# Moving the gamma LayerNorm's apply from two VectorE passes to two GpSimd passes and one VectorE pass

## The chip, the cores and the metric

The program runs on all 8 cores of one Trainium2 chip. Each core takes two of the 16 batch entries, and no core talks to another. The metric is the device time of the slowest core in microseconds (us). The engines are called as in the profile: PE is TensorE, DVE is VectorE, ACT is ScalarE, POOL is GpSimd, SP is the engine that issues the weight loads.

## The reference

The input is x of 16 x 2048 x 1024 floats. Three residual sublayers follow each other; the weights of the two FFNs are the same.

```python
def _layernorm(x, axis=-1, eps=1e-5): ...
x = x + 0.5 * _L0_ffn_ref(_layernorm(x), W1, b1, W2, b2, scale)
x = x + _L0_attn_ref(_layernorm(x), gamma, w_qkv, w_out)
x = x + 0.5 * _L0_ffn_ref(_layernorm(x), W1, b1, W2, b2, scale)
```

The FFN is a 1024 to 4096 to 1024 network with GELU, and with a small token-dependent term (rank 4) added to each of its two products. The attention has 8 heads of 128, is causal, and normalises its input once more by its root mean square and by gamma:

```python
l2 = jnp.sqrt(jnp.sum(x * x, axis=-1, keepdims=True))
xn = x / jnp.maximum(l2, 1e-12) * scale_norm * gamma
```

## The kernel before

Everything is held transposed: channels lie on the 128 partitions in 8 groups (cc), tokens along the free dimension. R is the residual in f32 (8 x 2048 columns), xn the normalised input in bf16, arena the 8 MB of hidden activations or of Q, K and V. The program handles one sequence of 2048 tokens after the other, and each as FFN 1, attention, FFN 2.

A list scheduler is not used. The builder calls emit in the order in which the work is written, each engine runs its own list strictly in that order, and waits come from the buffers' records of readers and writers. So the place of a call in the code sets the order on every engine.

ffn (from L741) runs two tiles of 1024 tokens (ti), each with an up projection (L762, GELU at L780) and two passes (nh) of 512 tokens: u, the small term's factor, is formed by 32 thin matmuls (L799), copied out of PSUM by ACT (L808), sent through DRAM and back, and beside it 256 matmuls of the down projection (L831) fill all eight PSUM banks. The pass ends with L845, ACT's bias (L852, into f32t) and DVE's residual add (L860). After each pass a hook is called.

ln_block (from L470) normalises one block of 512 tokens. PE sums x (L474) into PSUM bank 6; POOL or ACT squares each channel group into one of two halves of sqt (L488), and PE sums the squares (L494) into bank 7; ACT reads the sums (L504, L508), DVE and ACT form the variance and its inverse root in rows (L512 to L529), ACT sends two rows to DRAM and has them broadcast to 128 partitions as rep_a (scale) and rep_b (minus mean times scale). Then, for each of the 8 channel groups, two passes apply them, through the single buffer f32t. In the plain LayerNorm that a hook runs these are POOL's (L578, L582). With gamma fused they are DVE's (L585, L590): f32t = R * gamma * rep_a, then xn = rep_b * gamma + f32t.

The order around the change comes from FFN 1's hook, in its second tile:

```python
elif ti == 1 and nh == 0:
    ln_block(0, True, sq_eng='pool')
    ln_block(512, True, sq_eng='pool')
    ln_block(NT, True, sq_eng='pool')
elif ti == 1 and nh == 1:
    ln_block(NT + 512, True, sq_eng='pool')
```

So three blocks are normalised between the two down passes of the second tile, and the fourth behind the second pass, ahead of attention. Attention begins with V (L952): 16 tiles of 128 tokens, each 8 matmuls into one of two PSUM banks, copied out by DVE (L967); the first 12 tiles need no xn of the fourth block. These four calls, made for both sequences, are the only ones with gamma fused.

Of the kernel before, what the change touches and what calls it, by code (L numbers as in the profile page):

```python
# [251 lines left out]
def build(n_sub=3):  # L252
# [25 lines left out]
    p = Prog(nc)  # L278
    bufs = {}
    ctx = contextlib.ExitStack()  # L280
    with ctx:
        def sb(name, shape, dtype, nslots=1):
            t = ctx.enter_context(nc.sbuf_tensor(name, shape, dtype))
            bufs[name] = Buf(nslots)
            return t

        R = sb("R", [128, CC * S], F32, nslots=32)
# [5 lines left out]
        f32t = sb("f32t", [128, 512], F32)  # L293
        ln_t = f32t
# [17 lines left out]
        rep_a = sb("rep_a", [128, 512], F32)  # L312
        rep_b = sb("rep_b", [128, 512], F32)
# [4 lines left out]
        gamc = sb("gamc", [128, CC], F32)  # L318
# [21 lines left out]
        def B(name):  # L340
            return bufs[name]

        def rsl(cc, t0_, w=512):
            return R[:, cc * S + t0_: cc * S + t0_ + w]

        def rslot(cc, t0_):
            return cc * 4 + t0_ // 512

        def xsl(cc, t0_, w=512):
            return xn[:, cc * S + t0_: cc * S + t0_ + w]  # L350
# [27 lines left out]
        for name in ("b1c", "b2c", "gamc", "onesc", "onesf", "onesr", "negr", "ident",  # L378
# [3 lines left out]
                        deps=[ini_tok], group="scb", tag="scbc")  # L382
        B("scol").wrote(t_sc_ev)
        for src_s, dst_s, nm in ((o1s, o1sc, "o1sc"), (o2s, o2sc, "o2sc")):
            t = p.emit("dve", lambda e, src_s=src_s, dst_s=dst_s: e.tensor_scalar_mul(
                dst_s[:, :], src_s[:, :], scol[:, 0:1]),
                deps=[t_sc_ev, ini_tok], tag=nm)
# [78 lines left out]
        def layer_norm(t0, ntok, gamma_fused, bcast_pe=False, sq_eng="act"):  # L466
            for n0 in range(t0, t0 + ntok, 512):
                ln_block(n0, gamma_fused, bcast_pe, sq_eng)

        def ln_block(n0, gamma_fused, bcast_pe=False, sq_eng="act"):  # L470
            if True:
                ta = tb = None
                for cc in range(CC):
                    t_sa = p.emit("pe", lambda e, cc=cc, n0=n0: e.matmul(  # L474
                        ps[6][0:1, :], onesf[:, :], rsl(cc, n0), start=(cc == 0), stop=(cc == CC - 1)),
                        deps=B("R").deps_read(rslot(cc, n0)) + B("onesf").deps_read() +
                             (B("ps6").deps_write() if cc == 0 else []),
                        tag="sumx")
# [3 lines left out]
                for cc in range(CC):  # L482
# [4 lines left out]
                    else:  # L487
# [3 lines left out]
                        deps=B("R").deps_read(rslot(cc, n0)) + B("sqt").deps_write(pr), tag="sq")  # L491
# [5 lines left out]
                        deps=[t_sq] + B("onesc").deps_read() + (B("ps7").deps_write() if cc == 0 else []),  # L497
                        tag="sumx2")
# [6 lines left out]
                              deps=[ta] + B("srow_a").deps_write(), tag="mu")  # L505
# [3 lines left out]
                              deps=[tb] + B("srow_b").deps_write(), tag="ex2")  # L509
# [3 lines left out]
                             deps=[t_ea] + B("srow_c").deps_write(), tag="mu2")  # L513
# [3 lines left out]
                             deps=[t_eb, t_c], tag="var")  # L517
# [12 lines left out]
                              deps=[t_rsd, t_ea] + B("srow_c").deps_write(), tag="murstd")  # L530
# [3 lines left out]
                if bcast_pe:  # L534
                    t_b1m = p.emit("pe", lambda e: e.matmul(ps[6][:, :], onesr[:, :], srow_b[:, :],
                                                            start=True, stop=True),
                                   deps=[t_rsd] + B("ps6").deps_write() + B("onesr").deps_read(),
                                   tag="bcp1")
# [3 lines left out]
                    t_bc1 = p.emit("act", lambda e: e.copy(rep_a[:, :], ps[6][:, :]),  # L542
                                   deps=[t_b1m] + B("rep_a").deps_write(), tag="bcp1e")
# [5 lines left out]
                                   deps=[t_mr] + B("ps7").deps_write() + B("negr").deps_read(),  # L549
                                   tag="bcp2")  # L550
# [3 lines left out]
                    t_bc2 = p.emit("act", lambda e: e.copy(rep_b[:, :], ps[7][:, :]),  # L554
                                   deps=[t_b2m] + B("rep_b").deps_write(), tag="bcp2e")
                    B("ps7").read(t_bc2)
                    B("rep_b").wrote(t_bc2)
                else:
                    t_neg = p.emit("dve", lambda e: e.tensor_scalar_mul(srow_c[:, :], srow_c[:, :], -1.0),
                                   deps=[t_mr], tag="negmur")  # L560
# [7 lines left out]
                    t_bc1 = p.dma("act", rep_a[:, :], browL[0:1, 0:512].broadcast_to([128, 512]),  # L568
                                  deps=[t_o1] + B("rep_a").deps_write(), group="browL", tag="brL1i")
                    B("rep_a").wrote(t_bc1)  # L570
                    t_bc2 = p.dma("act", rep_b[:, :], browL[0:1, 512:1024].broadcast_to([128, 512]),
                                  deps=[t_o2] + B("rep_b").deps_write(), group="browL", tag="brL2i")
                    B("rep_b").wrote(t_bc2)
                ap_eng = "pool" if (sq_eng == "pool" and not gamma_fused) else "dve"
                for cc in range(CC):
                    xslot = rslot(cc, n0)
                    if not gamma_fused:
                        t_p1 = p.emit(ap_eng, lambda e, cc=cc, n0=n0: e.tensor_mul(  # L578
                            ln_t[:, :], rsl(cc, n0), rep_a[:, :]),
                            deps=[t_bc1] + B("f32t").deps_write() + B("R").deps_read(rslot(cc, n0)),  # L580
                            tag="lnap1")
                        t_p2f = lambda e, cc=cc, n0=n0: e.tensor_add(  # L582
                            xsl(cc, n0), rep_b[:, :], ln_t[:, :])
                    else:
                        t_p1 = p.emit(ap_eng, lambda e, cc=cc, n0=n0: e.scalar_tensor_tensor(  # L585
                            ln_t[:, :], rsl(cc, n0), gamc[:, cc:cc + 1], rep_a[:, :],
                            ALU.mult, ALU.mult),
                            deps=[t_bc1] + B("f32t").deps_write() + B("R").deps_read(rslot(cc, n0)) +
                                 B("gamc").deps_read(), tag="lnap1g")
                        t_p2f = lambda e, cc=cc, n0=n0: e.scalar_tensor_tensor(  # L590
                            xsl(cc, n0), rep_b[:, :], gamc[:, cc:cc + 1], ln_t[:, :],
                            ALU.mult, ALU.add)
                    B("rep_a").read(t_p1)
                    B("R").read(t_p1, rslot(cc, n0))
                    B("f32t").wrote(t_p1)
                    t_p2 = p.emit(ap_eng, t_p2f,
                                  deps=[t_bc2, t_p1] + B("xn").deps_write(xslot), tag="lnap2")
                    B("rep_b").read(t_p2)
                    B("f32t").read(t_p2)
                    B("xn").wrote(t_p2, xslot)  # L600
# [278 lines left out]
        def attn(ln_pre_blocks=0, hook=None):  # L879
            for n0 in range(ln_pre_blocks * 512, S, 512):  # L880
                ln_block(n0, True)
# [317 lines left out]
        for seq in range(BPC):  # L1199
            if n_sub >= 3:  # L1200
                first = (seq == 0)

                def ffn1_hook(ti, nh):
                    if ti == 0 and nh == 0:
                        if not first:
                            ln_block(NT, False, sq_eng='pool')
                            ln_block(NT + 512, False, sq_eng='pool')
                        t1_compute(NT)
# [6 lines that stand above are left out]
# [35 lines left out]
            else:  # L1250
# [9 lines left out]
               deps=B("srow_c").deps_write(), tag="trail_nop_act")  # L1260
# [47 lines left out]
```

How the kernel before makes its waits and increments, by code:

```python
            def run(engine_obj):  # L128
                hiwater = {}
                for op in oplist:
                    waits = {}
                    for d, m in op.deps:
                        if elided(e, d):
                            continue
                        s, v = d.sem, d.val
                        if m:
                            mo = margin_tok(d, op)
                            if mo is not None and mo.dma_group is None:
                                s, v = mo.tok.sem, mo.tok.val
                        assert s is not None, (e, op.tag, d.eng, d.idx)
                        if hiwater.get(s, 0) >= v:
                            continue
                        if waits.get(s, 0) < v:
                            waits[s] = v
                    for s, v in waits.items():
                        engine_obj.wait_ge(get_sem(s), v)
                        hiwater[s] = v
                        stats["waits"] += 1
                    ins = op.fn(engine_obj)
                    if op.needs_inc:
                        amt = 16 if op.dma_group is not None else 1
                        ins.then_inc(get_sem(op.tok.sem), amt)
                        stats["incs"] += 1
```

## Time and profile before

| what | value |
|---|---|
| timed runs | 4866.82 and 5091.31 us, median 4979.07 |
| the profiled execution | 4859.01 us |
| its span, slowest core (of 4834.5 to 4857.2) | 4857.2 us |
| PE busy | 3765.5 us, 78% of the span |
| ACT busy | 1206.7 us, 25% |
| POOL busy | 615.5 us, 13% |
| DVE busy | 597.4 us, 12% |
| chain that ended last, by engine | PE 64%, DMA 15%, ACT 5%, DVE 5%, issue 5%, POOL 5% |
| mean granted TensorE clock, eight cores | 0.872 to 0.875 of full speed |

The span runs from the first to the last instruction of one core; the 2 us beside it are the start and end of the program. An engine's busy time does not say what it holds up: the chain and the waits do. The eight cores do the same work and differ by half a per cent. The profile and all its rows are those of the slowest core, core 3.

### The profile page before, as it was taken

The numbers are of one execution on the slowest core, as the hardware profiler recorded it, in microseconds if no ns is written. First come the engines' busy times: TensorE is split into PE (matmuls) and PEld (weight loads), VectorE is DVE, ScalarE is ACT, GpSimd is POOL, SyncE is SP. The second block draws the span as 40 slices with busy tenths as digits, with TensorE's granted clock in tenths as the row PEclk, the third lists the DMA queues.
The fourth block names the chain that finished last, engine by engine and source line by source line (L and its number), as shares of the span: only waits on it lengthen the run. The fifth ranks groups of instructions, "written<-read, shape, count | busy, mean of one in ns | idle before, by whom it ended". The sixth has DMA issues, their size and how long they took to land.

```text
span 4857.2 us, 44500 instructions; the slowest of 8 cores (4834.5 to 4857.2 us)
## 1 busy us (share of the span) xinstructions
PE 3765.5 (78%) x14592; PEld 1310.6 (27%) x14592; DVE 597.4 (12%) x887; ACT 1206.7 (25%) x1873; POOL 615.5 (13%) x594
## 2 busy tenths in 40 slices
PE   5058999668888857896949849967878777597997
PEld 1013333222232212332313313322212212133333
DVE  3000001330031020000000010042112111100000
ACT  2012031015515502202212212210343344131121
POOL 0000001010010054002030040020110111610000
PEclk8579999878898978998969969988889989698998
DMA  9962423300100101252324213312010010023434
GB/s 191 196 134 59 121 58 87 87 14 18 42 11 18 33 11 40 61 153 71 92 74 122 70 42 94 79 57 76 20 37 14 18 31 18 14 61 96 113 81 130
DMA packets 436609, 333.30 MB, mean 69 GB/s; under 512 B 321130, under 2 KB 325612, under 8 KB 436388
## 3 DMA queue, kind: packets, MB, share of 16 engines
q1 hardware_dynamic: 394612, 252.00, 19.5%
q0 software_dynamic: 18144, 50.34, 5.2%
q10 hardware_dynamic: 23632, 28.12, 2.0%
q8 instruction: 126, 2.06, 0.2%
q14 instruction: 95, 0.78, 0.1%
HBM read 313.07 MB, written 42.45 MB: 73 GB/s over the span
## 4 chain that ended last, share of the span: by engine, by line
PE 64%; DMA 15%; ACT 5%; DVE 5%; issue 5%; POOL 5%; ACTq 1%; DVEq 0%; SPq 0%; POOLq 0%
PE ps L762 19%; PE ps L831 17%; PE ps L981 4%; PE ps L773 3%; PE ps L1051 3%; PE ps L1061 3%; PE ps L799 2%; PE ps L952 2%; PE ps L1028 2%; DVE nrm L903 2%; POOL sqt L488 2%; DMA browF<-srow_a 2%; PE ps L1154 2%; POOL xn L582 2%; POOL f32t L578 1%
## 5 line engine op out<-in xcount | busy, mean ns | idle before, releaser
L762 PE MATMUL ps<-xn,wb 128*128 128x512 bf16 x4096 | 986.3, 384 | 127.4 <-DMA wb<-w1s 113.2
L831 PE MATMUL ps<-arena,wb 128*128 128x512 bf16 x4096 | 895.7, 380 | 60.9 <-ACT u L808 51.0
L831 PEld LDWEIGHTS ps<-arena,wb 128*128 128x128 bf16 x4096 | 397.0, 98 | 558.6 <-issue 94.7
L780 ACT ACTIVATE arena<-ps,b1c 128x512 bf16<-128x512 f32 x512 | 351.4, 687 | 714.5 <-PE ps L773 700.3
L762 PEld LDWEIGHTS ps<-xn,wb 128*128 128x128 bf16 x4096 | 361.3, 98 | 618.8 <-issue 262.2
L1038 ACT ACTIVATE pb<-ps,negm 128x512 bf16<-128x512 f32 x640 | 419.2, 686 | 222.4 <-PE ps L1028 128.8
L860 DVE SCALAR_TENSOR_TENSOR R<-f32t,R 128x512 f32<-128x512 f32 x128 | 95.4, 746 | 2511.3 <-ACT f32t L852 1846.7
L488 POOL TENSOR_TENSOR sqt<-R 128x512 bf16<-128x512 f32 x160 | 176.1, 1131 | 1490.4 <-PE ps L494 827.3
L852 ACT ACTIVATE f32t<-ps,b2c 128x512 f32<-128x512 f32 x128 | 88.0, 687 | 1007.6 <-PE ps L845 899.0
L1051 PE MATMUL ps<-pb,onesc 128*1 128x512 bf16 x640 | 259.5, 406 | 89.7 <-ACT pb L1038 89.7
L494 PE MATMUL ps<-sqt,onesc 128*1 128x512 bf16 x192 | 92.1, 492 | 256.7 <-POOL sqt L488 249.2
L1028 PE MATMUL ps<-arena 128*128 128x512 bf16 x640 | 260.0, 416 | 30.6 <-ACT pb L1038 30.6
L889 POOL TENSOR_TENSOR sqt<-arena 128x512 bf16<-128x512 bf16 x128 | 132.2, 1038 | 1121.2 <-PE ps L981 954.7
L1061 PE MATMUL ps<-pb,arena 128*128 128x512 bf16 x640 | 266.5, 416 | 3.0 <-DVE arena L1089 3.0
L981 PE MATMUL ps<-xn,wb 128*128 128x512 bf16 x1024 | 234.3, 389 | 10.3 <-ACT arena L1000 10.3
L474 PE MATMUL ps<-R,onesf 128*1 128x512 f32 x384 | 197.3, 667 | 51.2 <-DMA R<-xT 36.7
L773 PE MATMUL ps<-t,e1z 4*128 4x512 bf16 x512 | 198.4, 388 | 0.0
L70 POOL DMA_DIRECT2D outT<-R x64 | 34.9, 546 | 1051.1 <-DVE R L860 1049.8
L723 PE MATMUL ps<-xn,o1c 128*4 128x512 bf16 x160 | 64.3, 563 | 128.0 <-ACT t L732 61.0
L1154 PE MATMUL ps<-arena 128*128 128x512 bf16 x512 | 131.8, 420 | 35.1 <-DVE arena L1089 27.0
L1051 PEld LDWEIGHTS ps<-pb,onesc 128*1 128x1 bf16 x640 | 50.7, 79 | 380.5 <-issue 380.5
L952 PE MATMUL ps<-arena,xn 128*128 128x512 bf16 x512 | 119.5, 398 | 43.0 <-DVE arena L967 43.0
(90 smaller groups left out, 2049.8 us busy)
## 6 DMA issues: line engine op xcount, KB each, us to landing
wb<-w2s SPq DMA_DIRECT2D x512, 256.0 KB, 2.6
wb<-w1s SPq DMA_DIRECT2D x256, 256.0 KB, 2.9
f32t<-browF ACTq DMA_DIRECT2D x64, 256.0 KB
outT<-R POOLq DMA_DIRECT2D x64, 256.0 KB, 3.3
arena<-w1T POOLq DMA_DIRECT2D x4, 2048.0 KB, 29.9
w1s<-arena SPq DMA_DIRECT2D x4, 2048.0 KB, 15.8
arena<-w2T POOLq DMA_DIRECT2D x4, 2048.0 KB, 25.7
w2s<-arena SPq DMA_DIRECT2D x4, 2048.0 KB, 16.3
```

What stands on the lines that cost most here:

```text
L488: sqf = lambda e, cc=cc, n0=n0, pr=pr: e.tensor_mul(sqt[:, pr * 512:(pr + 1) * 512], rsl(cc, n0), rsl(cc, n0))
L762: t_mm = p.emit("pe", lambda e, cc=cc, n0=n0, wt=wt, bank=bank: e.matmul(bank[:, :], wt[:, cc * 128:(cc + 1) * 128], xsl(cc, n0), start=(c ...
L773: t_c1 = p.emit("pe", lambda e, hc=hc, nh=nh, bank=bank: e.matmul(bank[:, :], e1z[:, hc * 128:(hc + 1) * 128], t1[:, nh * 512:(nh + 1) * 5 ...
L780: t_g = p.emit("act", lambda e, hc=hc, nh=nh, bank=bank: e.activation(h_act(hc, nh), bank[:, :], AF.Gelu, bias=b1c[:, hc:hc + 1]), deps=[t ...
L831: t_mm = p.emit("pe", lambda e, oc=oc, hc=hc, nh=nh, wt=wt, bank=bank: e.matmul(bank[:, :], wt[:, oc * 128:(oc + 1) * 128], h_act(hc, nh), ...
L952: t_mm = p.emit("pe", lambda e, cc=cc, tt=tt, bank=bank: e.matmul(bank[:, :], xn[:, cc * S + tt * 128: cc * S + (tt + 1) * 128], arena[:, ...
L981: t_mm = p.emit("pe", lambda e, cc=cc, nb=nb, wt=wt, bank=bank: e.matmul(bank[:, :], wt[:, cc * 128:(cc + 1) * 128], xsl(cc, nb * 512), st ...
L1028: t_s = p.emit("pe", lambda e, kcol=kcol, qcol=qcol, bank=bank, diag=diag: e.matmul(bank[:, :], arena[:, kcol:kcol + 128], arena[:, qcol:q ...
L1038: t_e = p.emit("act", lambda e, pslot=pslot, h=h, bank=bank: e.activation(pb[:, pslot * 512:(pslot + 1) * 512], bank[:, :], AF.Exp, bias=n ...
L1051: t_rs = p.emit("pe", lambda e, pslot=pslot, first=first, last=last, rsb=rsb: e.matmul(rsb[0:1, :], onesc[:, :], pb[:, pslot * 512:(pslot ...
L1061: t_pv = p.emit("pe", lambda e, vcol=vcol, pslot=pslot, first=first, last=last, ob=ob: e.matmul(ob[:, :], arena[:, vcol:vcol + 128], pb[:, ...
L1154: t_mm = p.emit("pe", lambda e, fc=fc, oc=oc, ocol=ocol, bank=bank: e.matmul(bank[:, :], arena[:, KT0 + fc * 1024 + oc * 128: KT0 + fc * 1 ...
```

## The change

For a block with gamma fused whose squares are POOL's, which is each of the four blocks of a sequence, the apply of one channel group is now three passes: POOL multiplies R by rep_a into f32t, POOL adds rep_b in place, and DVE multiplies the result by the group's column of gamma and writes xn in bf16. Since gamma is a factor of both terms, the result is the same up to rounding. The old branch stays in the code and is no longer reached.

```diff
                         t_p2f = lambda e, cc=cc, n0=n0: e.tensor_add(
                             xsl(cc, n0), rep_b[:, :], ln_t[:, :])
+                    elif sq_eng == "pool":
+                        t_p0 = p.emit("pool", lambda e, cc=cc, n0=n0: e.tensor_mul(
+                            ln_t[:, :], rsl(cc, n0), rep_a[:, :]),
+                            deps=[t_bc1] + B("f32t").deps_write() + B("R").deps_read(rslot(cc, n0)),
+                            tag="lnap0g")
+                        B("rep_a").read(t_p0)
+                        B("R").read(t_p0, rslot(cc, n0))
+                        B("f32t").wrote(t_p0)
+                        t_p1 = p.emit("pool", lambda e: e.tensor_add(
+                            ln_t[:, :], ln_t[:, :], rep_b[:, :]),
+                            deps=[t_p0, t_bc2], tag="lnap1g2")
+                        B("rep_b").read(t_p1)
+                        B("f32t").wrote(t_p1)
+                        t_p2f = lambda e, cc=cc, n0=n0: e.tensor_scalar_mul(
+                            xsl(cc, n0), ln_t[:, :], gamc[:, cc:cc + 1])
                     else:
                         t_p1 = p.emit(ap_eng, lambda e, cc=cc, n0=n0: e.scalar_tensor_tensor(
```

ln_t is another name of f32t. The second pass t_p2 is emitted on DVE as before.

POOL, from the weight preparation to the first attention, before. The squares (L488) of all four gamma blocks are one run of 32; L889 are the squares that attention takes of Q and K:

```order
L70 DMA arena<-wqkvT 128x2x3072 x4
L70 DMA arena<-woutT 128x4x1024 x2
L488 TENSOR_TENSOR sqt<-R 128x512 x32
L889 TENSOR_TENSOR sqt<-arena 128x512 x64
L488 TENSOR_TENSOR sqt<-R 128x512 x8
```

POOL in the changed kernel, around the end of block 0's apply and the squares of block 512. L585 is the new multiply, L592 the new add:

```order
L585 TENSOR_TENSOR f32t<-R,rep_a 128x512
L592 TENSOR_TENSOR f32t<-f32t,rep_b 128x512
L488 TENSOR_TENSOR sqt<-R 128x512 x8
L585 TENSOR_TENSOR f32t<-R,rep_a 128x512
L592 TENSOR_TENSOR f32t<-f32t,rep_b 128x512
```

Eight pairs now stand between the squares of one block and those of the next.

DVE before, at the end of block 0's apply and the statistics of block 512:

```order
L585 SCALAR_TENSOR_TENSOR f32t<-R,gamc,rep_a 128x512
L590 SCALAR_TENSOR_TENSOR xn<-rep_b,gamc,f32t 128x512
L512 TENSOR_TENSOR srow_c<-srow_a 1x512
L516 TENSOR_TENSOR srow_b<-srow_b,srow_c 1x512
L521 TENSOR_SCALAR srow_b<-srow_b 1x512
L529 TENSOR_TENSOR srow_c<-srow_a,srow_b 1x512
L559 TENSOR_SCALAR srow_c<-srow_c 1x512
L585 SCALAR_TENSOR_TENSOR f32t<-R,gamc,rep_a 128x512
```

DVE in the changed kernel, at the same place. L597 is the new multiply by gamma:

```order
L597 TENSOR_SCALAR xn<-f32t,gamc 128x512 x8
L512 TENSOR_TENSOR srow_c<-srow_a 1x512
L516 TENSOR_TENSOR srow_b<-srow_b,srow_c 1x512
L521 TENSOR_SCALAR srow_b<-srow_b 1x512
L529 TENSOR_TENSOR srow_c<-srow_a,srow_b 1x512
L559 TENSOR_SCALAR srow_c<-srow_c 1x512
L597 TENSOR_SCALAR xn<-f32t,gamc 128x512 x8
```

The statistics keep their place behind the block's apply; of the sixteen passes between them eight are left.

## Rows read from the trace of the kernel before

**Rows 1.** Groups by line, DVE then POOL: busy us, mean ns, idle before.

```profile
L585 DVE SCALAR_TENSOR_TENSOR f32t<-R,gamc,rep_a 128x512 f32<-128x512 f32 x64 | 52.6, 822 | 42.7 <-DMA rep_a<-browL 36.8
...
L521 DVE TENSOR_SCALAR srow_b<-srow_b 1x512 f32<-1x512 f32 x24 | 10.0, 415 | 2.6
...
L488 POOL TENSOR_TENSOR sqt<-R 128x512 bf16<-128x512 f32 x160 | 176.1, 1131 | 1490.4 <-PE ps L494 827.3 <-PE ps L723 250.7 <-PE ps L1154 212.3
...
L578 POOL TENSOR_TENSOR f32t<-R,rep_a 128x512 f32<-128x512 f32 x96 | 122.4, 1275 | 138.9 <-DMA rep_a<-browL 126.8
```

**Rows 2.** Waits of PE over the whole span: us in total, times, longest us.

```profile
PE ps L831 <- ACT u L808: 51.0, 2, 25.8
PE ps L952 <- DVE arena L967: 43.0, 2, 21.5
```

**Rows 3.** Timeline, first sequence: start us, us, engine, line, operation, [idle before].

```profile
844.13 1.26 DVE L590 SCALAR_TENSOR_TENSOR xn<-rep_b,gamc,f32t 128x512 bf16<-128x512 f32 x1 [2.18 <-DMA rep_b<-browL]
...
854.91 8.61 POOL L488 TENSOR_TENSOR sqt<-R 128x512 bf16<-128x512 f32 x6 [7.18 <-PE ps L494]
...
861.10 1.52 DVE L512 TENSOR_TENSOR srow_c<-srow_a 1x512 f32<-1x512 f32 x1
...
864.04 8.41 PE L799 MATMUL ps<-arena,o2c 128*4 128x512 bf16 x32
...
887.73 0.75 DVE L590 SCALAR_TENSOR_TENSOR xn<-rep_b,gamc,f32t 128x512 bf16<-128x512 f32 x1 [0.17 <-DVE f32t L585]
...
897.60 0.35 ACTq L70 DMA_DIRECT2D rep_b<-browL  x1
...
898.83 7.46 PE L831 MATMUL ps<-arena,wb 128*128 128x512 bf16 x21 [25.83 <-ACT u L808]
```

**Rows 4.** Timeline, second sequence, same place.

```profile
3215.91 1.49 DVE L590 SCALAR_TENSOR_TENSOR xn<-rep_b,gamc,f32t 128x512 bf16<-128x512 f32 x1 [1.95 <-DMA rep_b<-browL]
...
3270.20 49.59 PE L831 MATMUL ps<-arena,wb 128*128 128x512 bf16 x222 [25.18 <-ACT u L808]
```

**Rows 5.** Timeline ahead of attention, first sequence, then second.

```profile
981.75 0.59 ACT L508 ACTIVATE srow_b<-ps 1x512 f32<-1x512 f32 x1 [6.98 <-PE ps L494]
...
991.16 0.35 ACTq L70 DMA_DIRECT2D rep_b<-browL  x1
...
995.05 0.75 DVE L590 SCALAR_TENSOR_TENSOR xn<-rep_b,gamc,f32t 128x512 bf16<-128x512 f32 x1 [3.11 <-DMA rep_b<-browL]
...
1007.51 0.75 DVE L590 SCALAR_TENSOR_TENSOR xn<-rep_b,gamc,f32t 128x512 bf16<-128x512 f32 x1 [0.17 <-DVE f32t L585]
...
1009.01 26.55 PE L952 MATMUL ps<-arena,xn 128*128 128x512 bf16 x112 [21.52 <-DVE arena L967]
...
3364.47 0.75 DVE L590 SCALAR_TENSOR_TENSOR xn<-rep_b,gamc,f32t 128x512 bf16<-128x512 f32 x1 [2.49 <-DMA rep_b<-browL]
...
3377.00 0.75 DVE L590 SCALAR_TENSOR_TENSOR xn<-rep_b,gamc,f32t 128x512 bf16<-128x512 f32 x1 [0.24 <-DVE f32t L585]
```

**Rows 6.** Timeline of a plain LayerNorm that POOL applies, and the squares behind it.

```profile
1746.57 1.26 POOL L582 TENSOR_TENSOR xn<-rep_b,f32t 128x512 bf16<-128x512 f32 x1 [1.83 <-DMA rep_b<-browL]
...
1747.98 1.26 POOL L578 TENSOR_TENSOR f32t<-R,rep_a 128x512 f32<-128x512 f32 x1
...
1767.71 8.02 POOL L488 TENSOR_TENSOR sqt<-R 128x512 bf16<-128x512 f32 x8
...
1776.56 0.59 ACT L508 ACTIVATE srow_b<-ps 1x512 f32<-1x512 f32 x1 [24.03 <-PE ps L494]
```

**Rows 7.** Timeline: a residual add on DVE, and the POOL square waiting for it.

```profile
962.08 0.69 DVE L860 SCALAR_TENSOR_TENSOR R<-f32t,R 128x512 f32<-128x512 f32 x1 [0.88 <-ACT f32t L852]
...
963.04 1.04 POOL L488 TENSOR_TENSOR sqt<-R 128x512 bf16<-128x512 f32 x1 [99.52 <-DVE R L860]
```

**Rows 8.** Windows at PE's restart: PE, PEld, DVE, ACT, POOL busy us; PEclk, DMA share, GB/s.

```profile
890.00:905.00 15.00, 6.17 (x16) 2.07 (x17) 5.22 (x8) 3.26 (x6) 0.00 (x0) 0.52 0.20 55
905.00:920.00 15.00, 15.00 (x71) 6.83 (x70) 8.26 (x11) 0.00 (x0) 0.00 (x0) 1.00 0.48 142
```

## The prediction

> **What bounds the kernel now.** I read the groups by line first, to price the moved arithmetic. The first of the two DVE passes that apply a gamma LayerNorm block takes 0.82 us on average and runs 64 times [rows 1], the second as often. DVE as a whole is busy 12% of the span, so its load is no bound. TensorE (PE) carries the longest share of the chain that ended last, and what matters is where it stands still. The second view is therefore who waited for whom: PE waited 51.0 us in two waits for ACT's copies of u, and 43.0 us in two waits for DVE's copies of V [rows 2]. Both belong to the stage that the change touches. The third view is the timeline of that stage. I call the four blocks by their first token: 0, 512, 1024, 1536.
>
> *Place A*, between the two down projections of FFN 1's second tile: statistics of blocks 0, 512 and 1024 follow each other. Block 0's second apply pass starts when rep_b lands (844.13), DVE is done with block 0 only when it takes up block 512's mean at 861.10, its apply of block 512 ends at 888.48 (887.73 + 0.75), and only then can block 1024's variance start. ACT issues block 1024's broadcasts, the last at 897.60, and copies u behind them, so PE resumes at 898.83 after 25.83 us of idle time [rows 3]. The second sequence repeats it: 3215.91 to 3270.20 [rows 4]. *Place B*, ahead of attention: DVE applies block 1536 from 995.05 to 1008.26, and V's evacuations are queued behind it on DVE, so PE stands still 21.52 us until 1009.01 [rows 5]. So a longer apply lengthens the kernel at both places, in both sequences.
>
> **The change, part by part.** It removes 128 two-input DVE passes (8 blocks by 8 channel groups by 2) and adds 64 multiplies and 64 adds on POOL and 64 single-input multiplies on DVE. PE, the DMAs and ACT issue the same instructions.
>
> *Price of one channel group.* POOL's same multiply in the plain LayerNorm takes 1.26 us and the next dependent POOL instruction starts 1.41 us after it began (1747.98 minus 1746.57) [rows 1, 6]; the add takes 1.26 us. DVE's scalar multiply of 128x512 is not in the trace. The nearest row below is the 1x512 f32 scalar operation, 0.415 us, the nearest above the two-input pass, 0.75 us [rows 1, 5]; I take 0.42, since it is the same kind of operation over as many elements per partition, and keep 0.75. Now two handovers: there is one buffer f32t, so POOL's next multiply waits for DVE to have read it. DVE to POOL measured 0.27 us (962.08 + 0.69 to 963.04) [rows 7]; POOL to DVE is not shown, and the nearest row is DVE's wait for its own result, 0.17 us [rows 5]. I take 0.17 and 0.22 (the middle for the second), and keep zero and 0.27 for both as ends. One group then takes 1.41 + 1.26 + 0.17 + 0.415 + 0.22 = 3.47 us, against 1.78 before ((1007.51 - 995.05) / 7) [rows 5]. Counted from the landing of rep_b, POOL is free after 7 x 3.47 + 1.26 = 25.55 us and DVE after another 0.17 + 0.42, 26.15 us; before it was 13.21.
>
> The Trainium skill, "VectorE: DVE Perf Modes", section on the perf-mode tier table, lets an fp32 tensor_scalar in SBUF handle two elements per cycle where tensor_tensor handles one. By its fixed term of about 150 cycles my estimate is (256 + 151) / 0.96 GHz = 0.424 us; with the 0.75 us of a pass without that mode the total below would be about 15 us higher. No row shows this shape.
>
> *Place B.* POOL is idle there before the apply, and its squares come first in its queue. The last block is applied from the same moment and ends 26.15 - 13.21 = 12.9 us later; V's copies and PE follow one for one. Second sequence: (3377.00 + 0.75 - 3364.47) = 13.28 before, so again 12.9 [rows 5].
>
> *Place A.* Here the order decides. Before, POOL ran all squares without a stop (those of block 1024 from 854.91, while DVE applied block 0) [rows 3]. Now the squares of block 512 are queued on POOL behind the apply of block 0, those of 1024 behind the apply of 512; PE's sums of squares wait for them, then the statistics, then the next broadcast. Nothing overlaps any more. From block 0's rep_b at 844.13: apply 25.55; squares until ACT reads their sum 8.85 (1767.71 to 1776.56, a place where POOL is also the one waited for) [rows 6]; statistics and broadcast 13.3 (981.75 to 995.05) [rows 5]; apply of 512, 25.55; squares of 1024, 8.85; statistics to the last broadcast issue 9.41 (981.75 to 991.16) [rows 5]; u's copies and PE's start 1.23 (897.60 to 898.83) [rows 3]. Sum 92.74, so PE resumes at 936.9 instead of 898.83: 38.1 later. Second sequence: 3215.91 + 92.74 = 3308.65 against 3270.20, 38.4. The u matmuls (8.41 us from 864.04) [rows 3] now lie behind the last squares, 926.1 to 934.5, just inside ACT's chain, so they cost nothing; that cover is 2.4 us thin. They bring something back: at present PE restarts after its idle time at a granted clock of 0.52, the lower level (1.2 GHz), and is at 1.00 from 905 on [rows 8]; 21 matmuls took 7.46 us where 222 took 49.59 in the other sequence [rows 3, 4], a loss of 2.8 us. With u's matmuls immediately ahead, PE may be at full clock already. I take 1 us back in each sequence: 37.1 and 37.4.
> Block 1024's apply (926.25 + 13.3 to about 966) stays beside the down projection, which still has f32t unused until its end near 995; it costs nothing.
>
> A gain stands against this: DVE's passes took longer beside POOL's squares (six of them 8.61 us, against eight in 8.02 with no apply on DVE) [rows 3, 6]. The Trainium skill, "GPSIMD Engine Reference", Key points, says that POOL shares its SBUF interfaces with VectorE and contends with its two-input passes; by that rule the trace agrees and taking the passes off DVE frees the squares. It is in the sum already, since I took the undisturbed 8.85 us; with the disturbed rate of 8.61 / 6 per square it would be about 14 us more in total.
>
> **Sum.** 37.1 + 37.4 + 12.9 + 12.9 = 100.3 us. The profiled execution took 4859.01 us (span 4857.2), so about 4959 us, 2.06% more. The timed runs of before were 4866.82 and 5091.31, median 4979.07, so the profiled one lies 8 us under the lower; my figure is meant against the profiled and the lower one. 2%, about what a measurement of this kernel can tell from no change, is 97 us: the forecast lies almost on it.
>
> **Bounds.** Per sequence 21 group periods count. Handovers at zero give 3.09 us a period, 42 x 0.38 = 16 us less; the clock loss wholly recovered (2.8 instead of 1 in each sequence) 4 less: 4939. Handovers of 0.27 and a DVE pass of 0.75 give 3.96, 21 us more; u's matmuls wholly at 1.2 GHz (32 x 512 columns, 13.7 us) end 3 us behind ACT in each sequence, 6 more: 4986.
>
> **Rivals.**
> *Cheap handovers.* The engines' queues hide part of each handover and PE comes back at full clock: 4939 to 4950, say 4944. For it: own-engine waits of 0.17. Against: four semaphore steps per group, none of them seen at zero.
> *Dear handovers.* DVE's pass runs at one element per cycle or each wait costs 0.27: 4980. For it: DVE to POOL did cost 0.27. Against: 0.415 for the scalar operation.
> *Only B counts.* If u's copies were free of block 1024's statistics, place A would stay hidden behind the down projection and only 26 us would remain: 4885. Against: the 25.83 us wait for exactly this copy.
> *Not slower.* DVE, free of the two passes, takes up block 512's statistics as soon as its sums are there, ahead of 854.91 where the squares of 1024 go on, instead of at 861.10 [rows 3], and the statistics of all three blocks run on while POOL applies. PE would resume near 864 + 9.4 + 1.2 = 875, 24 us earlier at A, 13 later at B, net 11 less per sequence: 4837. This decides only if POOL's squares for 512 and 1024 stand ahead of its apply of block 0. The order shows them behind.
>
> **How the numbers follow.** Forecast as computed, 4950 to 4975: 0.60, of which 0.37 lies over the 2% line and 0.23 under it. Cheap handovers 0.18, dear 0.17, only B 0.03, not slower 0.02. Slower by over 2%: 0.37 + 0.17 = 0.54. Within 2%: 0.23 + 0.18 + 0.03 + 0.02 = 0.46, less the hundredth for faster by over 2%, which no case gives: 0.45. The range 4930 to 5000 takes in both bounds and a few microseconds between executions; about 0.1 is left outside.
>
> **What would show it.** Right: POOL instructions of this apply at 1.26 us and a period near 3.5; PE's waits for POOL's squares at A of about 30 us twice per sequence; PE's wait for V's first copy up from 21.5 to about 34; the squares of block 512 starting about 870. Wrong: squares running ahead of the apply, a period under 3.1 or over 4, or the stage from 811 to 1009 longer by less than 40 or more than 65 us. Elsewhere nothing should change.

## The result and the profile after

| | before | after |
|---|---|---|
| median of all timed runs | 4866.34 us (10 runs) | 4969.44 us (12 runs) |
| profiled execution | 4859.01 us | 4964.68 us |
| mean span of the eight cores | 4842.9 us | 4949.9 us |
| DVE busy | 597.4 us | 523.9 us |
| POOL busy | 615.5 us | 771.6 us |

The changed kernel takes 1.0221 times as long, with a 95% interval of 1.0201 to 1.024: 107 us more. DVE has 73 us less to do, and nothing is faster for it. Executions in which the cores of one die ran at a lower granted clock are left out of every ratio and mean in this text; the 5091.31 us among the two times shown ahead was one of them, and of three experiments (only_1536, squares_ahead, squares_on_act) there are no others, so of these only lengths measured on the four cores of the other die are used, and no whole time.

First the groups by line of the changed kernel, POOL's and then DVE's (busy us, mean ns, idle time before). The first row answers to L488 in [rows 1], the last three replace the row of L585 there.

```profile
L488 POOL TENSOR_TENSOR sqt<-R 128x512 bf16<-128x512 f32 x160 | 170.4, 1095 | 1328.1 <-PE ps L494 795.5 <-PE ps L738 243.3 <-PE ps L1169 217.4
...
L585 POOL TENSOR_TENSOR f32t<-R,rep_a 128x512 f32<-128x512 f32 x64 | 80.8, 1262 | 129.3 <-DMA rep_a<-browL 84.8 <-DVE xn L597 44.5
L592 POOL TENSOR_TENSOR f32t<-f32t,rep_b 128x512 f32<-128x512 f32 x64 | 80.7, 1261 | 23.2 <-DMA rep_b<-browL 14.9 <-POOL f32t L585 0.4
...
L597 DVE TENSOR_SCALAR xn<-f32t,gamc 128x512 bf16<-128x512 f32 x64 | 33.7, 527 | 241.2 <-POOL f32t L592 195.7 <-PE ps L846 45.5
```

Each of POOL's passes takes 1.26 us, as the plain LayerNorm's did. DVE's multiply, the shape of which no row of before showed, has a mean of 0.527 us. Behind its row stand 195.7 us in which DVE waited for POOL.

The waits of PE, one row of before and three of the changed kernel (us in total, times, longest). The second and third of the latter answer to [rows 2].

```profile
PE ps L494 <- POOL sqt L488: 249.2, 136, 33.5
```

```profile
PE ps L494 <- POOL sqt L488: 373.2, 144, 35.9
...
PE ps L967 <- DVE arena L982: 67.0, 2, 33.6
...
PE ps L846 <- ACT u L823: 3.5, 2, 2.1
```

The wait for u's copies has gone from 51.0 to 3.5 us, yet the kernel is slower: a wait for POOL's squares stands in its place, 124 us more of it. The wait for V's copies grew by 24.0 us. Together 124.0 - 47.5 + 24.0 = 100.5 us, which is about what the kernel lost. A reader who saw only that the wait for u vanished would have called it a gain.

Now place A in the timeline, in order: POOL, then DVE, ACT and PE, all of the changed kernel's first sequence. They answer to [rows 3]. (L592 is POOL's add, L597 DVE's multiply, L814 the u matmuls, L846 the down projection.)

```profile
836.59 1.26 POOL L592 TENSOR_TENSOR f32t<-f32t,rep_b 128x512 f32<-128x512 f32 x1 [1.70 <-DMA rep_b<-browL]
838.66 1.26 POOL L585 TENSOR_TENSOR f32t<-R,rep_a 128x512 f32<-128x512 f32 x1 [0.81 <-DVE xn L597]
840.06 1.26 POOL L592 TENSOR_TENSOR f32t<-f32t,rep_b 128x512 f32<-128x512 f32 x1
842.13 1.26 POOL L585 TENSOR_TENSOR f32t<-R,rep_a 128x512 f32<-128x512 f32 x1 [0.81 <-DVE xn L597]
...
862.11 8.64 POOL L488 TENSOR_TENSOR sqt<-R 128x512 bf16<-128x512 f32 x8
...
884.05 1.26 POOL L592 TENSOR_TENSOR f32t<-f32t,rep_b 128x512 f32<-128x512 f32 x1 [1.91 <-DMA rep_b<-browL]
...
909.91 8.64 POOL L488 TENSOR_TENSOR sqt<-R 128x512 bf16<-128x512 f32 x8
```

```profile
838.02 0.49 DVE L597 TENSOR_SCALAR xn<-f32t,gamc 128x512 bf16<-128x512 f32 x1 [9.09 <-POOL f32t L592]
```

```profile
871.58 0.59 ACT L508 ACTIVATE srow_b<-ps 1x512 f32<-1x512 f32 x1 [37.10 <-PE ps L494]
...
919.38 0.59 ACT L508 ACTIVATE srow_b<-ps 1x512 f32<-1x512 f32 x1 [37.59 <-PE ps L494]
...
928.89 0.35 ACTq L70 DMA_DIRECT2D rep_b<-browL  x1
```

```profile
863.39 0.58 PE L494 MATMUL ps<-sqt,onesc 128*1 128x512 bf16 x1 [31.97 <-POOL sqt L488]
...
911.20 0.58 PE L494 MATMUL ps<-sqt,onesc 128*1 128x512 bf16 x1 [31.56 <-POOL sqt L488]
...
919.08 8.39 PE L814 MATMUL ps<-arena,o2c 128*4 128x512 bf16 x32
...
930.12 52.27 PE L846 MATMUL ps<-arena,wb 128*128 128x512 bf16 x230 [2.11 <-ACT u L823]
```

One group starts 3.47 us after the other (838.66, 842.13). The squares of block 512 start at 862.11, when the last add of block 0 is through, and those of block 1024 at 909.91. PE stands still 31.97 and 31.56 us for them. Only 2.11 us are then left of the wait for u. These are the signs that the prediction had named: a period near 3.5 us, two waits of about 30 us, and squares that start 25.5 us after rep_b has landed (836.59 to 862.11). Place B, answering to [rows 5]:

```profile
1024.95 1.26 POOL L592 TENSOR_TENSOR f32t<-f32t,rep_b 128x512 f32<-128x512 f32 x1 [2.05 <-DMA rep_b<-browL]
...
1050.68 0.49 DVE L597 TENSOR_SCALAR xn<-f32t,gamc 128x512 bf16<-128x512 f32 x1 [2.98 <-POOL f32t L592]
...
1051.91 8.29 PE L967 MATMUL ps<-arena,xn 128*128 128x512 bf16 x31 [33.58 <-DVE arena L982]
```

The last group's multiply ends at 1051.17, 26.22 us after rep_b's landing, and PE waits 33.58 us instead of 21.52.

### The profile page after: what moved, and what is told of

Read it like the earlier page. It is cut to its first block, busy times and chain, and to the rows that moved or that the text cites. A ratio compares the mean times of both kernels' runs of the same rounds, so it can differ in the third digit from the quotient of the medians.

```text
span 4963.1 us, 44608 instructions; the slowest of 8 cores (4939.1 to 4963.1 us)
## 1 busy us (share of the span) xinstructions
PE 3771.1 (76%) x14592; PEld 1312.4 (26%) x14592; DVE 523.9 (11%) x823; ACT 1206.9 (24%) x1873; POOL 771.6 (16%) x722
## 4 chain that ended last, share of the span: by engine, by line
PE 62%; DMA 14%; POOL 7%; ACT 5%; issue 5%; DVE 4%; ACTq 1%; DVEq 0%; SPq 0%; POOLq 0%
PE ps L777 19%; PE ps L846 17%; PE ps L996 4%; PE ps L788 3%; PE ps L1066 3%; PE ps L1076 3%; PE ps L814 2%; PE ps L967 2%; PE ps L1043 2%; POOL sqt L488 2%; DVE nrm L918 2%; PE ps L1169 2%; POOL xn L582 1%; DMA browF<-srow_a 1%; POOL f32t L578 1%
## 5 line engine op out<-in xcount | busy, mean ns | idle before, releaser
L846 PE MATMUL ps<-arena,wb 128*128 128x512 bf16 x4096 | 893.9, 380 | 15.3 <-DMA wb<-w2s 11.1
L846 PEld LDWEIGHTS ps<-arena,wb 128*128 128x128 bf16 x4096 | 398.6, 98 | 509.7 <-issue 40.5
L488 POOL TENSOR_TENSOR sqt<-R 128x512 bf16<-128x512 f32 x160 | 170.4, 1095 | 1328.1 <-PE ps L494 795.5
L70 POOL DMA_DIRECT2D outT<-R x64 | 34.9, 546 | 1046.1 <-DVE R L875 1044.7
## 6 DMA issues: line engine op xcount, KB each, us to landing
arena<-w2T POOLq DMA_DIRECT2D x4, 2048.0 KB, 25.7
```

The lines of the kernel that those rows point to most:

```text
L488: sqf = lambda e, cc=cc, n0=n0, pr=pr: e.tensor_mul(sqt[:, pr * 512:(pr + 1) * 512], rsl(cc, n0), rsl(cc, n0))
L846: t_mm = p.emit("pe", lambda e, oc=oc, hc=hc, nh=nh, wt=wt, bank=bank: e.matmul(bank[:, :], wt[:, oc * 128:(oc + 1) * 128], h_act(hc, nh), ...
```

## The experiments

Times of whole executions scatter by some ten microseconds between executions and chips, which is as much as several of these effects. So the comparison goes by two stretches that every trace shows: A from the first bias-fold matmul of the first down pass (L845 before) to that of the second pass, and B from there to V's restart after its wait (L952 with DVE as releaser, or ACT where ACT makes the copies). Each figure is the mean over the eight cores, or over four of them for the three experiments named above, worked out from the start times in the timelines. Between the cores of one execution A + B of a sequence differs by up to 6.2 us (u_ahead_v_act). u_ahead_v_act and both_edits_again are the same kernel, profiled twice, and their sums differ by 1.7 us.

| kernel | A, first / second sequence | B, first / second | both, less before |
|---|---|---|---|
| before | 146.0 / 144.4 | 51.1 / 51.3 | |
| changed | 183.2 / 181.1 | 63.5 / 64.0 | +99.0 |
| only_1536 | 145.6 / 144.3 | 64.1 / 64.5 | +25.7 |
| only_a | 182.6 / 179.9 | 50.8 / 51.1 | +71.6 |
| squares_ahead | 172.8 / 170.3 | 63.8 / 64.1 | +78.2 |
| squares_on_act | 166.2 / 163.9 | 63.5 / 64.3 | +65.2 |
| three_on_dve | 153.2 / 151.9 | 54.6 / 55.4 | +22.1 |
| two_buffers | 169.4 / 169.6 | 57.8 / 58.0 | +61.9 |
| u_ahead | 121.5 / 119.7 | 51.2 / 51.5 | -49.0 |
| v_on_act | 145.8 / 144.1 | 34.6 / 35.3 | -33.0 |
| u_ahead_v_act | 120.9 / 121.6 | 34.6 / 35.3 | -80.3 |
| both_edits_again | 120.7 / 120.1 | 34.6 / 35.4 | -82.0 |
| new_u_ahead_v_act | 180.5 / 179.3 | 34.6 / 34.9 | +36.5 |

**Only block 1536.**

```diff
-                    elif sq_eng == "pool":
+                    elif sq_eng == "pool" and n0 == NT + 512:
```

> Only block 1536 gets the new arithmetic; blocks 0, 512 and 1024 keep the two VectorE passes. Theory (two places, each paying for itself): the stretch between the down passes keeps the length of before and the stretch from the end of the second down pass to V's restart grows from 51.3 to 63.7 us, as in the changed kernel; the whole execution is 25 us longer than before, about 4884 us, with the wait of PE for V's first copy at 34 us. Rival (the loss is a general one, from GpSimd and VectorE disturbing each other, not from these places): the time moves in proportion to the passes, a quarter of 106 us, with part of it outside this stretch.

Measured: A as before, B 13.1 us longer in each sequence. PE's waits on one of the four cores used:

```profile
PE ps L967 <- DVE arena L982: 68.4, 2, 34.7
...
PE ps L846 <- ACT u L823: 52.8, 2, 27.5
```

Both waits stand side by side: V's as in the changed kernel, u's as in the kernel before. The rival falls: the 13.1 us of B are the 12.9 forecast for this block alone, and nothing moved in A. Whether anything moved outside of the two stretches, this execution can't tell.

**Only blocks 0, 512 and 1024.**

```diff
-                    elif sq_eng == "pool":
+                    elif sq_eng == "pool" and n0 != NT + 512:
```

> Only blocks 0, 512 and 1024 get the new arithmetic, block 1536 keeps its two VectorE passes. Theory (two places that add up): the stretch between the down passes as in the changed kernel (182 us instead of 145), the one behind the second pass as before (51.3 us), 74 us more than before, about 4933. Rival (the places interact): anything off 74 by more than 5 us within the two stretches.

Measured: +71.6 us in the two stretches for 74 expected, in a profiled execution of 4930.53 us.

```profile
PE ps L494 <- POOL sqt L488: 376.1, 144, 43.2
...
PE ps L967 <- DVE arena L982: 43.7, 2, 22.2
...
PE ps L846 <- ACT u L823: 3.3, 2, 2.0
```

V's wait is back at 43.7, the squares' wait is the changed kernel's. 25.7 + 71.6 = 97.3 against 99.0: the two places add up.

**Squares ahead of the apply.** ln_block is cut into sums, statistics and apply; all the arithmetic is the changed kernel's.

```diff
-                        ln_block(0, True, sq_eng='pool')
-                        ln_block(512, True, sq_eng='pool')
-                        ln_block(NT, True, sq_eng='pool')
+                        s0 = ln_sums(0, 'pool')
+                        b0 = ln_stats(s0, True)
+                        s1 = ln_sums(512, 'pool')
+                        ln_apply(0, b0, True, 'pool')
+                        b1 = ln_stats(s1, True)
+                        s2 = ln_sums(NT, 'pool')
+                        ln_apply(512, b1, True, 'pool')
+                        b2 = ln_stats(s2, True)
+                        ln_apply(NT, b2, True, 'pool')
```

> The changed kernel with all its arithmetic, but the squares and sums of block 512 are emitted ahead of block 0's apply, and those of block 1024 ahead of block 512's; only GpSimd's order changes. Theory (half of the loss at place A is GpSimd's queue: squares stuck behind an apply): from rep_b of block 0 to PE's restart it takes 26.2 + 12.7 + 26.2 + 9.1 + 1.2 = 75 us instead of 93.5 (before: 54.7), so 18 us less in each sequence, 36 in all: about 4929 us. Rival (only the length of the apply counts, its order does not): 93 us again, 4965.

Measured: 20.8 us less than the changed kernel, where 36 were expected and the rival said none. The timeline on one of the four cores used shows where part of the rest went:

```profile
837.50 0.35 ACTq L70 DMA_DIRECT2D rep_b<-browL  x1
...
843.13 1.26 POOL L607 TENSOR_TENSOR f32t<-f32t,rep_b 128x512 f32<-128x512 f32 x1 [0.20 <-POOL f32t L600]
...
868.64 9.90 POOL L493 TENSOR_TENSOR sqt<-R 128x512 bf16<-128x512 f32 x8
...
869.88 1.51 DVE L522 TENSOR_TENSOR srow_c<-srow_a 1x512 f32<-1x512 f32 x1
...
871.50 1.34 DVE L526 TENSOR_TENSOR srow_b<-srow_b,srow_c 1x512 f32<-1x512 f32 x1
872.95 1.07 DVE L531 TENSOR_SCALAR srow_b<-srow_b 1x512 f32<-1x512 f32 x1
...
882.50 0.35 ACTq L70 DMA_DIRECT2D rep_b<-browL  x1
```

The squares of block 512 now hold back block 0's apply: its first add starts at 843.13, some 2 us after rep_b, issued at 837.50, could have landed. And the squares of block 1024 run from 868.64 beside DVE's statistics of block 512: the row of L522 takes 1.51 and that of L526 1.34 us instead of about 0.7, that of L531 1.07 instead of 0.41, so the next broadcast is issued 12.5 us after the apply has ended (869.96), not 9.1. These two make 5.5 of the 7.6 us that are missing in each sequence. The order does count, but I had priced the move as free.

**Squares on ScalarE.** This takes both side effects away.

```diff
+                    sqe = "act" if (gamma_fused and n0 in (512, NT)) else sq_eng
-                    if sq_eng == "act":
+                    if sqe == "act":
...
-                    t_sq = p.emit(sq_eng, sqf,
+                    t_sq = p.emit(sqe, sqf,
```

> The changed kernel, but the squares of blocks 512 and 1024 are ScalarE's, so that GpSimd's list holds nothing but the applies between the two down passes. Putting the squares ahead gave 21 us of the 36 expected; its trace shows the rest lost again, as the squares then delayed block 0's apply by 2 us and slowed VectorE's statistics beside them. Theory: without that, from rep_b of block 0 to PE's restart 75 us instead of 93.5 (squares ahead: 83), 18 per sequence, 36 in all, about 4929 on a span basis; table switches of ScalarE may add 1 to 3 us per block. Rival (the squares' place never mattered beyond those 21 us, because something else ends later): 4944 again.

Measured: 33.8 us less than the changed kernel, of 36 expected. Of the 2.2 us missing, 1.8 are the down projection's: PE now starts it after 25 us of idle time and not right behind u's matmuls, and from this restart to its bias fold it takes 58.5 and 57.8 us instead of 57.5 and 57.0 (means over the cores used).

```profile
826.86 5.31 ACT L486 ACTIVATE sqt<-R 128x512 bf16<-128x512 f32 x8 [6.52 <-DMA rep_a<-browL]
...
855.84 0.67 DVE L513 TENSOR_TENSOR srow_c<-srow_a 1x512 f32<-1x512 f32 x1
856.62 0.68 DVE L517 TENSOR_TENSOR srow_b<-srow_b,srow_c 1x512 f32<-1x512 f32 x1
```

ACT forms the squares of block 512 at 826.86, long before the statistics want them (855.84), and DVE's two rows take 0.67 and 0.68 us. The extra loads of ScalarE's tables that were feared did not come: the trace has 36 of them, as before. With the queue cleared, 166.2 - 146.0 = 20.2 us of the loss at A are left. That is about what the two applies themselves grew by, an estimate of 22 us: 26.2 each from the landing of rep_b, against 17.0 (844.13 to 861.10) and 13.2 before.

**Three passes, all on VectorE.**

```diff
-                        t_p0 = p.emit("pool", lambda e, cc=cc, n0=n0: e.tensor_mul(
+                        t_p0 = p.emit("dve", lambda e, cc=cc, n0=n0: e.tensor_mul(
...
-                        t_p1 = p.emit("pool", lambda e: e.tensor_add(
+                        t_p1 = p.emit("dve", lambda e: e.tensor_add(
```

> The changed kernel's three passes, all on VectorE. Theory (what costs is that the apply is GpSimd's, at 1.26 us a pass with two handovers and with the squares behind it): a group takes about 0.69 + 0.17 + 0.69 + 0.17 + 0.49 + 0.1 = 2.3 us against 1.78 before and 3.47 in the changed kernel, squares run ahead again; place A is 8 to 9 us longer than before, place B 4, in all 26 us more than before, about 4885. Rival (three passes instead of two is the cost, wherever they run): near the changed kernel, 4950 or more.

Measured: +22.1 us in the two stretches for 26 expected, against the changed kernel's 99.0. The rival falls: the third pass costs little, its engine and the queue it stands in cost much. The whole execution took 4905.83 us where 4885 were expected; the surplus lies outside of the two stretches and is taken up below.

```profile
L585 DVE TENSOR_TENSOR f32t<-R,rep_a 128x512 f32<-128x512 f32 x64 | 49.8, 777 | 42.9 <-DMA rep_a<-browL 37.1
L592 DVE TENSOR_TENSOR f32t<-f32t,rep_b 128x512 f32<-128x512 f32 x64 | 48.0, 751 | 25.1 <-DMA rep_b<-browL 18.9 <-DVE f32t L585 0.5
...
L597 DVE TENSOR_SCALAR xn<-f32t,gamc 128x512 bf16<-128x512 f32 x64 | 34.4, 538 | 10.3 <-DVE f32t L592 5.7 <-PE ps L846 2.0 <-PE ps L494 0.4
```

The same multiply and add that take 1.26 us on POOL take 0.777 and 0.751 on DVE, part of them beside POOL's squares.

**Two buffers.** In the gamma apply the groups use f32t and a second buffer in turn; to make room the row of minus ones goes, and ScalarE gives a broadcast of the prologue its sign.

```diff
+        f32u = sb("f32u", [128, 512], F32)
...
+                        lt_, ltn = (f32t, "f32t") if cc % 2 == 0 else (f32u, "f32u")
```

> The changed kernel with a second f32 buffer, used in turn by the channel groups, so that GpSimd's next multiply does not wait for VectorE (a broadcast of the prologue gets its sign from ScalarE to make room for it). Theory (0.66 us of the 3.47 us period is the round trip through VectorE): the period becomes 2.81 us, each apply 4.6 us shorter, place A 9 and place B 4.6 us shorter per sequence, 28 in all: about 4937. Rival (VectorE's multiply, now beside GpSimd's passes, contends with them and gives it back): GpSimd's passes grow over 1.26 us and the time stays at 4955 or more.

Measured: 37.1 us less than the changed kernel, more than the 28 expected, and 4926.6 us in all.

```profile
837.13 1.26 POOL L593 TENSOR_TENSOR f32t<-f32t,rep_b 128x512 f32<-128x512 f32 x1 [2.47 <-DMA rep_b<-browL]
838.35 1.26 POOL L586 TENSOR_TENSOR f32u<-R,rep_a 128x512 f32<-128x512 f32 x1
838.56 1.33 DVE L598 TENSOR_SCALAR xn<-f32t,gamc 128x512 bf16<-128x512 f32 x1 [10.15 <-POOL f32t L593]
839.75 1.26 POOL L593 TENSOR_TENSOR f32u<-f32u,rep_b 128x512 f32<-128x512 f32 x1
840.97 1.26 POOL L586 TENSOR_TENSOR f32t<-R,rep_a 128x512 f32<-128x512 f32 x1
```

The period is 2.62 us (838.35 to 840.97), not 2.81: POOL's passes on different buffers follow each other without a gap. DVE's multiply takes 1.33 us beside them instead of 0.49, and POOL's stay at 1.26. The rival saw the contention rightly, but not who pays: DVE has the time. Waiting for DVE and for its own results thus cost POOL 0.85 us of each 3.47.

**u's copies ahead**, on the kernel before: the statistics and apply of block 1024 are emitted behind u's copies and transfers.

```diff
-                        ln_block(NT, True, sq_eng='pool')
+                        late.append((NT, ln_sums(NT, 'pool')))
...
                     B("u4").wrote(t_uin)
+                    while late:
+                        ln0, lst = late.pop(0)
+                        ln_apply(ln0, ln_stats(lst, True), True, 'pool')
```

> The kernel before with its arithmetic; the copies of u and their two transfers are put ahead of block 1024's statistics and apply on every engine's list. Theory (PE stands still at place A only because ScalarE's copies of u are queued behind block 1024's broadcasts, which wait for block 512's apply): the 25.8 and 25.2 us waits go to about 1 us, 49 us in all, about 4810. Rival (the down projection then starts beside the apply and stops again for something else, PSUM or weights): less than half of it.

Measured: 49.0 us less in the two stretches, 49 expected. On the slowest core 0.9 us are left of the 51.0 us of waits for u. Of the two long waits only the other one remains:

```profile
PE ps L972 <- DVE arena L987: 42.5, 2, 21.6
```

The profiled execution took 4816.3 us.

**V's copies on ScalarE**, on the kernel before.

```diff
-                    t_ev = p.emit("dve", lambda e, col0=col0, bank=bank: e.tensor_copy(
+                    v_eng = "act" if hh == 0 else "dve"
+                    t_ev = p.emit(v_eng, lambda e, col0=col0, bank=bank, v_eng=v_eng: (
+                        e.copy if v_eng == "act" else e.tensor_copy)(
```

> The kernel before; V's copies out of PSUM in the first half of the heads are ScalarE's instead of VectorE's. Theory (PE stands still at place B only because the copies are queued behind block 1536's apply on VectorE): the first copy starts when ScalarE has issued the last broadcast, 991.7 instead of 1008.2, so the wait falls from 21.5 to about 5 us, the tiles that need block 1536 arrive just after its apply has ended, and the execution is 33 us shorter, about 4826. Rival (block 1536's tiles then wait instead): about the same time as before.

Measured: the mean span of the eight cores is 4814.3 us against 4842.9, 28.6 less for 33 expected; the one time is 4832.81. In the two stretches it is 33.0 us less, as expected; the other 4 lie outside of them.

**Both edits**, and once more with more rounds.

> Both of these edits on the kernel before. Theory: they add up, 82 us less than before, about 4777, 1.7% faster. Rival (the second wait hides part of the first): between 4790 and 4810.

> The kernel before with u's copies ahead and V's copies on ScalarE, once more with more rounds. Theory: 0.983 of the time before, 80 us less. Rival: less than 1% once more executions are compared.

Measured on one chip: 4785.53, 4775.82, 4768.65 and 4780.43 us, mean 4777.6; the kernel before beside them eight times, 4851.24 to 4870.32, mean 4859.6. The ratio of the means is 0.983, and from the scatter of the two groups I work out a 95% interval of about 0.981 to 0.985. So 82 us, as expected: this version beats both kernels.

**Both edits on the changed kernel.**

> Both of these edits on the changed kernel. Theory (in the changed kernel PE waits at place A for GpSimd's squares, not for u's copies, and at place B the tiles of block 1536 would wait for its longer apply): place A gains only 2 to 3 us per sequence, place B 18, in all 41 less than the changed kernel, about 4924, so that the new arithmetic costs about 147 us where both covers are gone, against 106 as submitted. Rival (the change only lengthens the same two waits, which these edits remove): the same time as the same edits on the kernel before, 4777 to 4800.

Measured: 4914.12 us, A 180.5 and 179.3. The rival falls. Against both edits on the kernel before (mean spans 4777.3 and 4762.0) its mean span of 4894.3 is 117 to 132 us longer, where the changed kernel as submitted loses 107. The stretches separate it better. A and B together are 116.8 and 118.5 us longer than with both edits on the kernel before (two profiles), all of it in A. B is as short as there, but V, from its restart to PE's next work, takes 35.8 and 35.7 us where it takes 25.9 to 26.6 with both edits on the kernel before. With V the new arithmetic costs 135 to 138 us here, against 98.7 as submitted and 147 expected. How V loses its 9 us shows on one core:

```profile
1008.50 21.25 PE L987 MATMUL ps<-arena,xn 128*128 128x512 bf16 x85 [5.70 <-ACT arena L1003]
1030.26 0.38 PE L987 MATMUL ps<-arena,xn 128*128 128x512 bf16 x1 [0.51 <-DVE xn L614]
1033.73 0.38 PE L987 MATMUL ps<-arena,xn 128*128 128x512 bf16 x1 [3.10 <-DVE xn L614]
1037.21 7.61 PE L987 MATMUL ps<-arena,xn 128*128 128x512 bf16 x25 [3.10 <-DVE xn L614]
```

The tiles of block 1536 need each group as it comes: PE waits 0.51 and twice 3.10 us for single groups, in step with POOL's period, and not for the end of the apply as I had reckoned.

## Why the prediction was right and where it was off

Both places and their mechanism were as forecast. *The price of a group*, 3.47 us, was measured at 3.47, and part of that is luck. Two of its terms were off by 0.07 us each and cancelled: DVE's multiply took 0.49 us where I took 0.42 (838.02), and DVE to POOL 0.15 (838.51 to 838.66) where I took 0.22; POOL to DVE was 0.17 as taken. In the second sequence of this core POOL to DVE took 0.11 at place A, and the period there is 3.40. *The chain at place A* was put at 92.74 us from rep_b's landing to PE's restart and measured 93.53 (836.59 to 930.12). Its steps: apply 25.52 for 25.55; squares until ACT reads their sum 9.47 for 8.85, since the second and third of them, at 1.22 and 1.48 us instead of 1.03, run beside DVE's last multiply and its statistics; statistics and broadcast 12.47 for 13.3; second apply 25.86; squares 9.47 again; then 9.51 and 1.23. *Place B* was put at 12.9 more, the experiment alone gave 13.1, and the changed kernel 12.4 and 12.7.

In the two stretches the forecast of 100.3 us compares with 99.0 measured. The timed ratio makes it 107. The 7 to 8 us between lie outside them: before, the rest of the mean span is 4842.9 - 392.8 = 4450.1 us, in the changed kernel 4949.9 - 491.8 = 4458.1. I do not put them down to the change, because the rest of one and the same kernel moves by more: u_ahead_v_act has a rest of 4777.3 - 312.5 = 4464.8 and both_edits_again, which is that kernel profiled again, one of 4762.0 - 310.8 = 4451.2. only_a, with three quarters of the new arithmetic, has 4915.2 - 464.4 = 4450.8, and three_on_dve, with none of POOL's part, 4883.1 - 415.0 = 4468.1. The interval of the ratio, 1.0201 to 1.024, begins at 98 us, so it does not exclude the 99.0 either. These runs do not settle whether a few of them belong to the change.

The step that failed is the comparison in the sum: "my figure is meant against the profiled and the lower one". It set 4959 us against 4859.01 and 4866.82 and left the median beside it, 4979.07, as it stood. Against that median 4959 is 20 us less, no change or a slight gain, while the text says slower; the kernel came out 2.21% slower. With ten runs the median of before is 4866.34, 112.7 us under the one that the prediction printed. So the anchor that the text chose was right and the median was not, and with two runs 225 us apart the prediction should have said outright that the median stood for neither, and given its figure as a ratio, 1.0206. The change itself, 100.3 us, was off by 1.3 in the stretches it was worked out for.

"Elsewhere nothing should change" put at nothing what the mean span shows as 8 us and what, as said, cannot be told from scatter. The measured median of 4969.44 is 10 us over my number: 3 are the difference of the medians, 103.1 us for 100.3, and 7 the anchor, one execution of 4859.01 where the median is 4866.34.

The chances were close to even between slower and no change, because the sum fell 3 us over the line of 2%; that the ratio came out on its upper side by as little is no merit of the forecast. The mechanism was surer than that; what was open were a few tenths of a microsecond taken 42 times. "Dear handovers" was wrong in its cause: of the 64 handovers from POOL to DVE on this core 63 took 0.11 to 0.18 us and one 0.53, and DVE to POOL took 0.14 or 0.15. The cover that I called thin, 2.4 us for u's matmuls, was 2.11. The clock gave back about the 1 us taken: from PE's restart to its bias fold the down pass took 57.5 and 57.0 us in the two sequences against 58.6 and 58.2 before (means of eight cores). It was not back on every core. After the 2.11 us wait of this one the granted clock was 1.00 from 925 to 930 and 0.70 from 930 to 935, and the first 21 matmuls took 7.0 us; at ten of the sixteen restarts of the eight cores they took 5.3.

Two readings in the prediction need a word. The 2.8 us that it gives as the clock's loss are reckoned against the row of 222 matmuls, which itself begins after an idle time and at a granted clock of 0.50 (3270 to 3272), so that row is no measure of full speed. And the 8.61 us for six and 8.02 for eight, given there for "DVE's passes", are the lengths of POOL's squares; what DVE's passes did is seen in 1.26 us at 844.13 against 0.75 at 887.73 [rows 3]. Nor did POOL run its squares "without a stop": it waited 7.18 us for PE ahead of block 1024's.

"Not slower" was never tested as such: it needs the next block's statistics ahead of the apply as well, and broadcasts that do not wait for rep_a. squares_on_act comes nearest and still stands 65 us above before.

## What to carry to other kernels

Before moving elementwise work to an engine that is idle on average, look at what else that engine's list holds at the same place: here eight squares behind each apply turned two overlapped blocks into a chain. Taking load off an engine that was 12% busy gave nothing, and when a wait disappears from the list of waits, see what took its place. The gain lay in the order of two lists: what PE waits for should not be queued behind what waits for a DMA.

## What the runs showed of the hardware

DVE's multiply of 128x512 by a column took 0.49 us alone and 1.33 beside POOL's two-input passes (two_buffers), while POOL's stayed at 1.26. Beside POOL's squares both sides paid: before, DVE's two-input passes took 1.26 us instead of 0.75, and six squares 8.61 us where eight take 8.02 alone [rows 3, 6]. DVE's rows of 1x512, on a single partition, stretched too, from about 0.7 to 1.34 and 1.51 us (squares_ahead). POOL's own passes followed each other at 1.22 us when they used different buffers (837.13 to 838.35) and at 1.40 when the second read what the first had written (838.66 to 840.06).
